# Moving three small norm matmuls per token tile from before to behind the V projection

## The reference

```python
q = (x @ Wq).reshape(b, s, 2 * H, hd)          # x is the layer norm of the input
k = (x @ Wk).reshape(b, s, 2 * NUM_KV_HEADS, hd)
v = (x @ Wv).reshape(b, s, NUM_KV_HEADS, 2 * hd)
q = rope(q).transpose(0, 2, 1, 3) * scaling
k = rope(k).transpose(0, 2, 1, 3)
scores = jnp.einsum('bhqd,bhkd->bhqk', q, k)
probs = jax.nn.softmax(scores.astype(jnp.float32), axis=-1)
w = probs[:, :, 0] - lam * probs[:, :, 1]
attn = jnp.einsum('bhqk,bhkd->bhqd', w, v)      # then rms norm, @ Wo, residual
out = e0 * fw[:, 0:1] * m0 + e1 * fw[:, 1:2] * m1   # the experts, then residual
```

## Time and profile before

| what | value |
|---|---|
| median of three timed runs | 4460.68 us (4460.55 to 4461.32) |
| the profiled execution, its own time | 4457.12 us |
| its span, slowest core (core 4) | 4455.6 us |
| spans of the other cores | 4419.7 to 4434.4 us |
| PE busy / DVE busy / ACT busy | 3207.8 / 1108.8 / 2552.9 us |
| mean granted TensorE clock, core 4 | 0.824 of full speed |

### The profile page before, as it was taken

One profiled execution on the slowest core, in us unless ns is written; L12 is line 12 of the kernel. 1 busy time (PEld: TensorE's weight loads), 2 busy tenths in 40 slices (PEclk: granted clock), 3 DMA queues, 4 the chain that ended last, 5 costly groups with the idle time before them and its releaser, 6 DMA issues.

```text
span 4455.6 us, 48438 instructions; the slowest of 8 cores (4419.7 to 4455.6 us)
## 1 busy us (share of the span) xinstructions
PE 3207.8 (72%) x16039; PEld 952.3 (21%) x16100; DVE 1108.8 (25%) x2063; ACT 2552.9 (57%) x3590; POOL 179.0 (4%) x212
## 2 busy tenths in 40 slices
PE   2525535668888888888888888888888888715598
PEld 0213211221221212222222222222222222203332
DVE  3637743331111111111111111111111111124422
ACT  1313310007777777777777878787878777703321
POOL 0213310000000000000000000000000000000000
PEclk9868867786887867887888989898989898957789
DMA  2223321100000000000000000000000000022201
GB/s 73 75 84 106 109 79 35 25 23 1 2 3 2 3 2 2 3 2 3 2 3 2 3 2 3 2 3 2 3 2 3 2 3 2 3 75 83 71 33 43
DMA packets 96042, 108.20 MB, mean 24 GB/s; under 512 B 57780, under 2 KB 70198, under 8 KB 95800
## 3 DMA queue, kind: packets, MB, share of 16 engines
q1 hardware_dynamic: 88888, 84.11, 6.7%
q0 software_dynamic: 6912, 20.98, 1.7%
HBM read 84.09 MB, written 20.97 MB: 24 GB/s over the span
## 4 chain that ended last, share of the span: by engine, by line
PE 45%; ACT 24%; DVE 10%; issue 9%; DMA 9%; POOL 2%; ACTq 1%; DVEq 0%; SPq 0%; POOLq 0%
ACT pt L709 22%; PE psA L687 11%; PE psS L674 10%; PE psZ L697 7%; PE pp L299 5%; PE psE L1051 3%; PE psZ L616 2%; DMA wst<-w 2%; PE psE L1056 2%; PE psZ L628 1%; DVE gmax L460 1%; DMA xqb<-xq 1%; POOL pb_ L313 1%; DMA wst<-wo 1%; DMA wstage<-wq 1%
## 5 line engine op out<-in xcount | busy, mean ns | idle before, releaser
L709 ACT ACTIVATE pt<-psS,mneg_bc 128x1024 bf16<-128x1024 f32 x2048 | 2198.4, 1110 | 640.9 <-PE psS L679 636.4
L687 PE MATMUL psA<-pt,Vtm 128*64 128x512 bf16 x1984 | 881.7, 444 | 457.3 <-ACT pt L709 420.0
L692 PE MATMUL psA<-pt,Vtm 128*64 128x512 bf16 x1984 | 919.2, 463 | 0.0
L701 PE MATMUL psZ<-pt,ones64b_s 128*64 128x512 bf16 x1984 | 883.9, 446 | 0.0
L679 PE MATMUL psS<-Qfm,Kfm 32*128 32x512 bf16 x2048 | 881.4, 435 | 0.0
L697 PE MATMUL psZ<-pt,ones64b_s 128*64 128x512 bf16 x1984 | 881.0, 444 | 0.0
L674 PE MATMUL psS<-Qfm,Kfm 32*128 32x512 bf16 x2048 | 879.9, 435 | 1.2 <-DVE Lmat L570 1.2
L687 PEld LDWEIGHTS psA<-pt,Vtm 128*64 128x64 bf16 x1984 | 221.6, 112 | 1077.0 <-issue 1077.0
L608 DVE RECIPROCAL zrbuf<-psZ 128x512 f32<-128x512 f32 x64 | 214.9, 3358 | 889.8 <-PE psZ L729 889.8
L674 PEld LDWEIGHTS psS<-Qfm,Kfm 32*128 32x128 bf16 x2048 | 184.2, 92 | 1094.8 <-issue 1094.8
L299 PE MATMUL pp<-wbuf,hfmb 128*128 128x512 bf16 x1245 | 390.6, 483 | 13.1 <-ACT hfmb L284 7.8
(11 more groups left out here) (143 smaller groups left out, 2300.1 us busy)
## 6 DMA issues: line engine op xcount, KB each, us to landing
xbuf<-x SPq DMA_DIRECT2D x32, 512.0 KB
xbuf<-xq SPq DMA_DIRECT2D x16, 512.0 KB
hfm_s<-hfmb POOLq DMA_DIRECT2D x32, 256.0 KB, 3.2
hfmb<-hfm_s SPq DMA_DIRECT2D x32, 256.0 KB
xqb<-xq SPq DMA_DIRECT2D x16, 512.0 KB
wst<-w SPq DMA_DIRECT2D x32, 256.0 KB
out<-ybuf POOLq DMA_DIRECT2D x16, 512.0 KB, 2.9
wstage<-wq SPq DMA_DIRECT2D x16, 256.0 KB
```

Source lines behind the costliest of these rows:

```text
L687: T(lambda t, jj=jj, pm=pm, d=d, aset=aset: t.matmul(psA[aset][0:64, :], Vtm[:, jj * D + d * 64: jj * D + d * 64 + 64], pt[:, pm * 1024: p ...
L692: T(lambda t, jj=jj, pm=pm, d=d, aset=aset: t.matmul(psA[aset][64:128, :], Vtm[:, jj * D + d * 64: jj * D + d * 64 + 64], pt[:, pm * 1024 ...
L701: prog.op("tensor", lambda t, jj=jj, pm=pm, aset=aset: t.matmul(psZ[aset][64:128, :], ones64b[:, :], pt[:, pm * 1024 + 512: pm * 1024 + 1024],
L709: A(lambda sc, p=p: sc.activation(pt[:, p * 1024: p * 1024 + 1024], psS[:, p * 1024: p * 1024 + 1024], AF.Exp, bias=mneg_bc[:, 0:1], scale ...
```

## The change

The three slices of a round are written behind the round's projection instead of ahead of it.

```diff
-        for _ in range(3):
-            if nslices:
-                nslices.pop(0)()
         ppb = t % 2
         mm = project_tile(hfmb[hb], wbuf, ppb, None,
                           [(s_ld, ld), (s_dve, max(c_wv, last_pp_read[ppb])),
                            (s_act, last_pp_act[ppb])])
         last_vproj[hb] = mm
         last_hfmb_use[hb] = (s_pe, mm)
+        for _ in range(3):
+            if nslices:
+                nslices.pop(0)()
         cv = V(lambda v, t=t, ppb=ppb, hb=hb: v.tensor_copy(
```

## The result

The changed kernel takes 4323.09 us (median of 10 runs, 4304.22 to 4349.73) against 4459.8 us before (10 runs, 4454.29 to 4464.19). The ratio is 0.9698, 95% interval 0.9677 to 0.9719: 3.0% faster. The forecast was 4323.

A forecast was written before the change was run, and what follows sets the result against it. V stage bound by PE and DVE waiting in turn, plus a lowered clock: 31 x (10.19 - 5.66) = 140.4, + 0.5 - 1.7 - 1.4 = 137.8 us less, giving 4323 us; range 4301 to 4345, 8 of 10 in 4300 to 4352.

The forecast's parts named there:

- The new round: V stage, one projection's start to the next: 5.66 us instead of 10.19, over 31 rounds.
- the six terms: Parts of the V stage's new round: 3.45 + 0.38 + 0.11 + 0.86 + 0.55 + 0.31 = 5.66 us.
- The sixth: V stage, projection's start until PE is free for the norm matmuls: 3.45 us at full clock, from the K pass.
- The clock: V stage projections: every burst at full clock after 1.3 us of idle; half clock would cost 1.70 us a round.
- DVE's cover: V stage: two squares done about 2.5 us into the next projection, needed at 3.45; 1 us to spare.
- The loads: V stage tile loads: 2.6 us on average, 2.9 at most, stay hidden with 4.8 us to spare.
- Start and end: V stage's edges: start gains 0.5 us, slow first burst loses 1.7, end costs 1.4, each once.
- The power limit: Dense matmuls on all cores lose full clock: V stage round 0.8 us longer, 25 us in all, 4348 us; chance 3%.
- The third rival: V stage: a power limit takes full clock from dense matmuls on all cores; 4348 us; chance 3%.
- The attention: Attention behind the V stage: three slow groups of 7.5 us may come or go, +-22 us.
- The slower rival: Attention groups take 51.83 instead of 44.37 us; over 18.5 more make it slower, 25 more give 4509 us; chance 2%.

The follow-up runs named there:

- e1: The changed kernel with each round's copy ahead of its squares on DVE; 4430.6 us in one run, rounds of 10.11 to 10.26 us.
- e7: The changed kernel with 92 of the 96 norm slices left out; 4247.3 us in one run.
- e2: The kernel before with idle 128x512 matmuls added on PE while it waits for DVE; 4400.7 us, ratio 0.9874 to the kernel before.
- e4: The kernel before with two of a round's three slices moved behind the projection, one left ahead; 4315.0 us in one run.
- e5: The changed kernel with three buffers for squares and three norm rows instead of two each; 4267.9 us, ratio 0.9602 to the kernel before.
- e3: The kernel before with one of a round's three slices moved behind the projection, two left ahead; 4360.6 us in one run.

## Why the prediction was right

The mechanism was read from the two sides of the waits, and e1 shows that it was the right one: the same PE order without the squares made ahead brings nothing.

- *The new round.* Forecast 5.66, measured 5.76. Of the six terms, five came out within 0.01 us: 0.38 for the matmul, 0.10 to the reduce (0.11), 0.86 to the square, 0.55 to the matmul, 0.31 to the projection. The sixth, from the projection's start to the next matmul, is 691.34 - 687.78 = 3.56 where I took 3.45 from the K pass. There transposes follow a projection, here norm matmuls with a single column of weights, which carry a wait on DVE, already fulfilled. The wait by itself does not cost it: in e7 projections carry fulfilled waits too and follow each other in 703.12 - 699.67 = 3.45 us, and the second norm matmul, which carries its own, starts 0.21 us after the first. That leaves the shape, which no run isolates. It is 3.4 us over the stage.
- *The clock.* Taken as full, and it is 1.00 on every core. Its price, 1.70 us a round, is 1.76 in e2. One of the two supports was weak, though: the burst of the earlier trace rows that ran full after 3.60 us of idle was one of several, which do not agree: six tiles later in the same pass a burst of the same 16 matmuls took 5.30 us after the same idle (last section). That 1.3 us of idle is short enough, and even 1.59, was shown by the change and by e4, not by that row.
- *DVE's cover.* Forecast 1 us: the last square was to be done 2.5 us into the projection and needed at 3.45. In the profile it starts 689.89 - 687.78 = 2.11 us into it and is 0.40 long. Right, and e5 used nearly all of what DVE had left.
- *The loads.* Never waited for in a steady round; only the first one is, as foreseen.
- *Start and end.* The first projection starts at 679.83 on core 3, the chain begins 868.25 - 860.68 = 7.57 us after the last one's start (forecast 7.45). The stage's end, forecast near 864, comes at 866.4 to 871.6 on the eight cores, where it was 1000.4 to 1006.8: 134.1 us sooner in the mean, of 137.8 forecast. Of the missing 3.7 the sixth term makes 3.4. The start brought less than the 0.5 us taken: the first projection starts 2.9 to 3.1 us after the stage's first square, where it was 3.2, and the slow first burst takes 5.6 to 6.5 us, 2.0 to 2.9 more than a full one, where I took 1.7. Against that the old round was 10.23 us in the mean and not 10.19: the row at 680.38 in the earlier trace rows holds 15 of the projection's 16 matmuls, so its true start lies earlier.
- *The power limit.* The third rival said that dense matmuls on all cores lose their full clock; e5 keeps PE busy 99.21 of 100 us on its slowest core and is granted 1.00, on all eight cores, and its projection takes 3.63 us. So it fell for the V stage. But the chance given to it was not idle: in the changed kernel's profile two cores are granted 0.81 in the experts' stage, at 84.02 us of work in 85, and two in the attention (last section). The Trainium skill ("TensorE: Matmul & The Clock Gate", "Seeing it yourself") gives 13/16 of the clock as the rule once three cores of a die run dense matmuls; 0.81 is that share, but e5's eight cores ran them at 1.00, so the rule does not hold throughout here.
- *The attention.* Allowed for as +-22 us, and it was needed: the ten runs spread by 45.5 us. Those of before spread by 9.9 beside them, but by 45.9 on the experiments' first chip, so a wide spread needs no change. The total came out on the forecast to 0.1 us because the slowest core's extra was nearly alike in both medians (136.7 us between the medians, 134 in the stage); that agreement is luck.

The slower rival, a lost step in the attention, exists as a mechanism: nine of core 3's 63 group steps are over 47.5 us, on the slow core of before it was six. It was priced right as far too small.

## What to carry to other kernels

When two engines wait for each other in turn, find the instruction on which each side waits, and see that the work which the other side needs stands ahead of it; a new order on the waiting engine alone brings nothing if the other one still makes its part behind the wait (e1). Price the clock apart from the gap: here 4.7 us of gap cost another 1.7 us in the burst behind it, and filling the gap with idle matmuls is the test (e2).

## What the runs showed of the hardware

The clock falls without any long idle. In e1, whose gaps are those of the kernel before, PE's idles in a round are 2.12, 0.81 and 0.81 us with single norm matmuls between, and the clock is 0.78 in the mean; the kernel before starts its bursts at 0.51; in the K pass a burst ran at full speed after 3.60 us of unbroken idle and eight short transposes, and another, after 3.59 us and eight such transposes, took 5.30 us for the same 16 matmuls:

```profile
548.78 0.61 PE L278 MATMUL trb<-identb_s,ropeo 128*128 128x128 bf16 x8 [3.59 <-DVE ropeo L321]
549.23 5.30 PE L299 MATMUL pp<-wbuf,hfmb 128*128 128x512 bf16 x16
```

So the single longest gap does not tell which level a burst gets: in e3, with 1.81 and 0.81 us of idle a round, both levels occur.

The granted clock was 0.81 for a while, which is neither of the two levels. This is the experts' stage of the changed kernel, cores 2 and 4 of one execution: a stretch and one group of matmuls of each.

```profile
4100.00:4185.00 85.00, 84.02 (x240) 26.99 (x245) 19.57 (x18) 13.81 (x14) 3.23 (x6) 0.81 0.09 36
4156.77 2.27 PE L1051 MATMUL psE<-w1T,h_all 128*128 128x512 bf16 x8
```

```profile
4100.00:4185.00 85.00, 84.05 (x292) 29.41 (x298) 24.68 (x23) 15.37 (x15) 4.29 (x8) 1.00 0.12 47
4151.95 1.90 PE L1051 MATMUL psE<-w1T,h_all 128*128 128x512 bf16 x8
```

Core 3 had 0.81 from 4136 to 4186 us; from its first to its last group of matmuls the stage took 201.6 us on core 2, 195.5 on core 3 and 187.1 on core 4. Cores 0 and 1 had 0.81 in stretches between 2065 and 2225 us, in the attention. Cores 4 to 7, the other die, never had it for as long as 4 us, nor had any core in the eight other profiles. What brings it on is not shown.

The long attention groups run mostly at half clock. Two stretches of the kernel before, an ordinary group and a long one on core 4:

```profile
1327.48:1371.85 44.37, 36.01 (x198) 9.13 (x196) 6.78 (x7) 35.02 (x34) 0.53 (x1) 0.88 0.01 2
1371.85:1423.68 51.83, 47.88 (x198) 9.73 (x196) 6.78 (x6) 35.92 (x34) 0.53 (x1) 0.60 0.01 2
```

The same 198 matmuls and 34 operations of ACT take 7.46 us more at 0.60 than at 0.88. The slowest core ends 9.7 to 58.9 us behind the first in 18 runs of before, and 18.8 to 53.9 in 11 runs after. Why a core falls into such groups, mostly in its first sixteen, and another doesn't, stays open; no experiment here was made for it. The slowest core's lag, 25.5 us in the median of the 18, is what it could be worth.
